# A causal mask by VectorE inside its row maximum, and a head's score tail beside the next head's masks

## The reference

```python
scores = jnp.einsum('bhqd,bhkd->bhqk', q, k) / np.sqrt(hd)
scores = scores + _alibi_causal_mask(S, scores.dtype)   # k <= q: -(q - k), else -1e30
probs = jax.nn.softmax(scores, axis=-1)
out = jnp.einsum('bhqk,bhkd->bhqd', probs, v)
```

## Time and profile before

| | |
|---|---|
| Median of 3 runs | 1567.94 us (1562.91 to 1567.96) |
| Span of the profiled execution, first to last instruction | 1560.2 us |
| Between the median and the span | 7.7 us |
| TensorE busy | 1472.0 us, 94% |
| TensorE weight loads | 946.3 us, 61% |
| VectorE busy | 1277.9 us, 82% |
| ScalarE busy | 1147.2 us, 74% |
| GpSimd busy | 858.0 us, 55% |

### The profile page before, as it was taken

The page is one execution under the profiler, slowest core; times in us unless marked ns, Lnnn a source line. Parts: engine busy times, 40 slices in busy tenths (PEclk is TensorE's granted clock), DMA queues, the critical chain, the costliest instruction groups (busy, mean ns, idle before and its releaser), DMA issues.

```text
span 1560.2 us, 56229 instructions
## 1 busy us (share of the span) xinstructions
PE 1472.0 (94%) x21476; PEld 946.3 (61%) x21476; DVE 1277.9 (82%) x3030; ACT 1147.2 (74%) x2464; POOL 858.0 (55%) x924
## 2 busy tenths in 40 slices
PE   6888999999999999999999999999999999999996
PEld 5555656666666666666666666656666656666653
DVE  6777888888888888888888888888888888888836
ACT  2477777778777777777877877777777777777762
POOL 2124556556556556655655665565665565566454
PEclk9799999999999999999999999999999999999988
DMA  5344555555455555455555545555545555554521
GB/s 170 99 150 127 171 156 173 152 170 157 149 178 155 175 153 166 143 168 167 157 180 152 160 146 170 166 160 157 165 142 167 175 150 178 154 169 139 157 73 50
DMA packets 197298, 239.73 MB, mean 154 GB/s; under 512 B 22462, under 2 KB 147782, under 8 KB 197030
## 3 DMA queue, kind: packets, MB, share of 16 engines
q1 hardware_dynamic: 196972, 236.07, 49.4%
q10 hardware_dynamic: 64, 0.07, 0.0%
HBM read 134.25 MB, written 100.73 MB: 151 GB/s over the span
## 4 chain that ended last, share of the span: by engine, by line
PE 62%; DVE 10%; DMA 9%; issue 6%; SPq 6%; ACT 3%; POOL 2%; POOLq 0%; DVEq 0%; ACTq 0%
PE ps L599 26%; PE ps L753 11%; PE ps L748 8%; PE ps L807 6%; DMA qk_d<-qk_st 5%; PE ps L802 5%; DVE mxp L1089 3%; DMA kz<-qk_d 2%; PE ps L768 2%; PE ps L662 2%; SPq L412 2%; DVE ve_c L1014 1%; DVE zr L1101 1%; DVE st_c L1000 1%; SPq L429 1%
## 5 line engine op out<-in xcount | busy, mean ns | idle before, releaser
L1089 DVE TENSOR_REDUCE mxp<-ps 128x4 f32<-128x512 f32 (+1 forms) x1536 | 842.8, 592 | 160.5 <-PE ps L768 155.6
L863 ACT ACTIVATE prob<-ps 128x512 f32<-128x512 f32 (+1 forms) x1536 | 732.6, 525 | 121.8 <-PE ps L753 116.4
L753 PE MATMUL ps<-qs,kz 50*128 50x128 f16 (+2 forms) x3584 | 405.9, 240 | 12.9 <-DVE mxp L1089 10.5
L768 PE MATMUL ps<-kz,qs 49*128 49x128 f16 (+1 forms) x4096 | 410.5, 231 | 0.1
L753 PEld LDWEIGHTS ps<-qs,kz 50*128 50x128 f16 x3584 | 261.4, 94 | 88.7 <-ACT prob L863 31.1
L768 PEld LDWEIGHTS ps<-kz,qs 49*128 49x128 f16 x4096 | 286.3, 95 | 3.8 <-DVE mxp L1089 1.8
L1347 POOL TENSOR_TENSOR om<-oc,rz 128x512 f32<-128x512 f32 x62 | 77.4, 1270 | 329.9 <-DMA rz<-rz_d 329.9
L807 PE MATMUL ps<-prob,va 128*32 128x384 f32 (+2 forms) x3072 | 237.6, 381 | 0.0
L748 PE MATMUL ps<-mk 64*128 64x256 bf16 x1024 | 198.6, 274 | 36.0 <-DMA kz<-qk_d 11.3
L802 PE MATMUL ps<-prob,va 128*32 128x128 f32 x4096 | 209.6, 277 | 0.6 <-DVE qk_st L1021 0.6
L764 PE MATMUL ps<-mk 64*128 64x256 bf16 x1024 | 201.0, 276 | 5.4 <-DVE mxp L1089 3.4
(11 more groups left out here) (157 smaller groups left out, 2870.6 us busy)
## 6 DMA issues: line engine op xcount, KB each, us to landing
qk_d<-qk_st SPq DMA_DIRECT2D x128, 256.0 KB, 2.8
ou_d<-ou SPq DMA_DIRECT2D x124, 256.0 KB, 2.3
qs<-qk_d SPq DMA_DIRECT2D x256, 96.0 KB, 2.4
kz<-qk_d SPq DMA_DIRECT2D x256, 96.0 KB, 2.5
xa<-in_L_attn_x SPq DMA_DIRECT2D x32, 512.0 KB, 5.2
qk_d<-qk_st SPq DMA_DIRECT2D x128, 128.0 KB, 3.4
xc<-in_L_attn_x SPq DMA_DIRECT2D x32, 512.0 KB, 4.1
oc<-ou_d SPq DMA_DIRECT2D x31, 512.0 KB, 4.9
```

The source lines that it names most:

```text
L753: x_ = mm(bank[:, col:col + w * P], kz[rows, h // 2, kt * P:(kt + 1) * P], qs[rows, h // 2, qt * P:(qt + w) * P], start=(n > 0), stop=(n > ...
L768: x_ = mm(bank[:, col * P:(col + w) * P], qs[rows, h // 2, qt * P:(qt + 1) * P], kz[rows, h // 2, kt * P:(kt + w) * P], start=(n > 0), sto ...
L863: nc.scalar.activation(prob[:, h % 8, at:at + w], ps[:, ST + n, 0:w], ACT.Exp, scale=1.0 / FS).then_inc(s["exp_done"], 1)
L1089: v.tensor_reduce(mxp[:, g % 2, at, first:first + apart * (BLOCKS[n] - 1) + 1:apart], bank.rearrange("p (m k) -> p m k", k=P), AX.X, ALU.m ...
```

## The change

- TensorE no longer adds a mask to the row scores. Row scores come in four whole tiles, one for each block of 128 queries, each with all its keys: 256 columns (bank 0), 512 (bank 1), 384 and 128 (bank 2). They take 4 matmuls instead of 10.
- VectorE adds the mask and takes the maximum of a tile in one instruction, `tensor_tensor_reduce` with add and max, four for each head. It reads the scores from PSUM and the mask from SBUF, writes the masked scores to a new tile `masked` (bf16), which nothing reads, and the maximum of each row straight into `mxt`. `mxp` and the four `rmax` steps of a batch are gone. `mt` waits for the last maximum of its group by `mx_read`.
- The tail of a head's transposed scores (256 columns, chunk 2) moves from part 2 of its own slot to part 0 of the next, between the two masks of the next head. ScalarE's exp of it comes first in the next slot.
- The constant mask has 1024 columns instead of 768.

```diff
-        MOVES = [6, 2, 2]
-        ROWS_AT = [[(0, 0, 1, 0), (1, 1, 1, 1), (2, 2, 1, 2), (3, 3, 1, 3)], [(3, 0, 3, 1), (2, 1, 1, 0)],
-                   [(1, 0, 1, 0), (2, 0, 1, 1)]]
+        ROW_TILES = [[(1, 0)], [(3, 0)], [(2, 0), (0, 3 * P)]]
+        MASKED = {3: 0, 2: 4 * P, 0: 7 * P, 1: 8 * P}
...
             def mt(b, n):
                 dst = to("mt", n, b)
-                wait(pe, "mxt_ready", b * 4 + n + 1)
+                wait(pe, "mx_read", b * 48 + 12 * (n + 1))
...
+            def row_score(b, pos, n, m):
+
+                h = pos ^ 1
                 rows = slice(HALF * (h % 2), HALF * (h % 2) + MX_ROWS)
...
+                qt, col = ROW_TILES[n][m]
+                w = (qt + 1) * P
+                x_ = mm(ps[:, MX + n, col:col + w], qs[rows, h // 2, qt * P:(qt + 1) * P],
+                        kz[rows, h // 2, 0:w], start=True, stop=True)
+                if m == len(ROW_TILES[n]) - 1:
                     x_.then_inc(s["mx_ready"], 1)
...
+            def masks_part(i, t):
+
+                bm, pos = max_at(i, t)
+                bp, hp = head_before(i, t)
+                if live(i):
...
+                    wait(pe, "exp_done", i * 48 + 3 * t - 2)
+                    mask(t, 0)
+                if live(bp):
+                    score(bp, hp, 2, 0)
+                if live(i):
+                    mask(t, 1)
+                if live(bm):
...
+                    wait(pe, "mx_read", bm * 48 + 3 * pos - 2)
+                    row_score(bm, pos, 0, 0)
+
+            def diagonal_part(i, t):
+
+                bm, pos = max_at(i, t)
+                if live(i):
+                    score(i, t, 0, 0)
+                if live(bm):
+                    wait(pe, "mx_read", bm * 48 + 3 * pos - 1)
+                    row_score(bm, pos, 1, 0)
+                if live(i):
+                    for m in range(1, 4):
+                        score(i, t, 0, m)
+
+            def past_part(i, t):
+
+                bm, pos = max_at(i, t)
+                if live(i):
+                    wait(pe, "exp_done", i * 48 + 3 * t - 1)
+                if live(bm):
+                    wait(pe, "mx_read", bm * 48 + 3 * pos)
+                for m in range(2):
+                    if live(i):
+                        score(i, t, 1, m)
+                    if live(bm):
+                        row_score(bm, pos, 2, m)
...
+            def exp_part(i, t, n):
+
+                b, h = (i, t) if n else head_before(i, t)
+                if live(b):
+                    exp(b, h, (n + 2) % 3)
...
-                bank = ps[:, MX + n, 0:BLOCKS[n] * P]
-                first, apart = MX_AT[n]
-                v.tensor_reduce(mxp[:, g % 2, at, first:first + apart * (BLOCKS[n] - 1) + 1:apart],
-                                bank.rearrange("p (m k) -> p m k", k=P), AX.X, ALU.max).then_inc(s["mx_read"], 1)
-
-            def rows_max(b, g):
-                wait(dve, "mx_read", b * 48 + 12 * (g + 1))
-                wait(dve, "mt_ready", b * 4 + g - 3)
-                v.tensor_reduce(mxt[:, g, :], mxp[:, g % 2].rearrange("p h (m k) -> p (h m) k", k=4), AX.X,
-                                ALU.max).then_inc(s["mxt_ready"], 1)
+                wait(dve, "mx_read", b * 48 + 3 * pos + n - 2)
+                if pos % 4 == 0 and n == 0:
+                    wait(dve, "mt_ready", b * 4 + g - 3)
+                for qt, col in ROW_TILES[n]:
+                    w = (qt + 1) * P
+                    x_ = v.tensor_tensor_reduce(masked[:, MASKED[qt]:MASKED[qt] + w], ps[:, MX + n, col:col + w],
+                                                mk[:, S - w:S], 1.0, -3e38, ALU.add, ALU.max,
+                                                mxt[:, g, 4 * at + qt:4 * at + qt + 1])
+                x_.then_inc(s["mx_read"], 1)
```

More of the change, by code:

```diff
@@ L66 @@
 DVE_AT = {
-    0: [(0, "rmax", 1, 0), (0, "ot", 0, -2), (3, "bn_c", 0, -2), (3, "ot", 1, -2)],
+    0: [(0, "ot", 0, -2), (3, "bn_c", 0, -2), (3, "ot", 1, -2)],
     1: [(3, "bn_c", 1, -2)],
@@ L77 @@
     12: [(3, "zs", 2, -2)],
-    13: [(1, "zs", 3, -2), (1, "rmax", 0, 1)],
+    13: [(1, "zs", 3, -2)],
 }
@@ L165, in build @@
         vst = sb("vst", [P, QT, D], F32)
-        mxp = sb("mxp", [P, 2, 4, 16], F32)
+        masked = sb("masked", [P, 10 * P], BF16)
         mxt = sb("mxt", [P, 4, 16], F32)
@@ L740, in moe, with mask @@
                 products(dst, pairs).then_inc(s["moe_ready"], 1)
+            def mask(h, u):
+                half = slice(HALF * (h % 2), HALF * (h % 2) + HALF)
+                mm(ps[:, ST, :].rearrange("p (t k) -> p t k", t=QT)[:, :, HALF * u:HALF * u + HALF], mask_key(u)[half],
+                   EYE[half].rearrange("p (t k) -> p t k", t=QT), start=(u == 0), stop=False)
             def score(b, h, n, m):
                 rows = slice(HALF * (h % 2), HALF * (h % 2) + ST_ROWS)
-                half = slice(HALF * (h % 2), HALF * (h % 2) + HALF)
@@ L746, in score @@
[L746 to L753, removed]
-                            qs[rows, h // 2, qt * P:(qt + w) * P], start=(n > 0), stop=(n > 0 or m == 5))
@@ L755, in score @@
-                if m == (MOVES[n] if n < 2 else 1) - 1:
+                kt, qt, w = CHUNK[n][m]
+                col = sum(c[2] for c in CHUNK[n][:m]) * P
+                last = m == len(CHUNK[n]) - 1
+                x_ = mm(ps[:, ST + n, col:col + w * P], kz[rows, h // 2, kt * P:(kt + 1) * P],
+                        qs[rows, h // 2, qt * P:(qt + w) * P], start=(n > 0), stop=(n > 0 or last))
+                if last:
                     x_.then_inc(s["st_ready"], 1)
-            def row_score(b, pos, h, n, m):
+            def row_score(b, pos, n, m):
+                h = pos ^ 1
@@ L793, in weigh @@
+            def both(i, t, n):
+                (masks_part, diagonal_part, past_part)[n](i, t)
             def weigh(b, g):
@@ L821, in drain @@
             def drain():
+                wait(pe, "exp_done", NB * 48 - 3)
+                score(LAST, H - 1, 2, 0)
                 weigh(LAST, 3)
@@ L938, in one @@
                 for t in range(SLOTS):
-                    play(i, t, ACT_END if i == LAST else ACT_AT, steps, lambda i, t, n: live(i) and exp(i, t, n))
+                    play(i, t, ACT_END if i == LAST else ACT_AT, steps, exp_part)
             hf_a_, hh_a_ = turned("ta", "ta_ready", 0, hf_a, hh_a, "hfa_ready", "hha_ready", "hla_ready",
@@ L954, in drain @@
             def drain():
+                exp(LAST, H - 1, 2)
                 sums_out(LAST, 3)
@@ L1449, in constants @@
     row = at % HALF
-    keys = [np.where(at[None, :] < row[:, None] + HALF * u, NEG, 0.0) for u in range(2)]
     queries = [np.where(at[None, :] > row[:, None] + HALF * u, NEG, 0.0) for u in range(2)]
     eye = np.tile(np.where(row[:, None] == np.arange(HALF)[None, :], 1.0, 0.0), (1, 4))
-    mask = np.concatenate([*keys, *queries, eye], axis=1).astype(np.float32)
+    future = np.where(np.arange(-3 * P, P)[None, :] > at[:, None], NEG, 0.0)
+    mask = np.concatenate([future, *queries, eye], axis=1).astype(np.float32)
     kaug = np.full((2, 8, 512), FS, np.float16)
```

55 lines of the change are left out of this document (16 added, 39 removed).

## The result

The kernel after takes 1604.42 us (median of 4 runs, 1602.89 to 1605.07) against 1566.55 us for the one before: ratio 1.0249, 95% interval 1.0224 to 1.0275. The forecast was 1606 us. The number is right by luck, and most of the reasons behind it are wrong: the price per head that the forecast gave VectorE isn't there, and a cost that it took as nothing is.

A forecast was written before the change was run, and what follows sets the result against it. TensorE paced the longest stretch, and VectorE would become the longer there. +1.1 us a batch x 31 = +34, plus 3 and 1.5 once, made +38 us and 1606 us; likeliest case 1580 to 1650, 8-in-10 range 1515 to 1700.

The forecast's parts named there:

- What leaves TensorE: Score matmuls: the old third part of a head goes, saving TensorE 0.11 to 0.17 us a head.
- What VectorE gets: Row maxima: a head costs VectorE 1.90 us instead of 1.54 (bounds 1.61 and 2.54), by a separate short instruction per tile.
- Stretch A: Batch part from 718.24 to 743.94, paced by TensorE: VectorE becomes the longer, 26.4 us, +0.7 a batch.
- first rival: Whole kernel: the maximum costs VectorE nothing extra, 1.61 us a head, TensorE stays the bound; 1505 to 1530 us, chance 0.28.
- Stretch B: Batch part from 743.94 to 753.21, TensorE and VectorE alternating: dearer maxima before the q and k products, +0.4 us.
- Stretch C: Batch part from 753.21 to 763.89, waiting on stores and loads: VectorE's extra work is covered by DMAs, no change.
- What is moved: Tail's exp first in ScalarE's next slot: ScalarE, busy 35.56 of 45.65 us, takes it; 0 us taken.
- VectorE busy over 93%: Sign for the forecast in the profile after: VectorE's busy share, 82% before, rises over 93%.
- its wait under 50 us: Sign for the forecast in the profile after: VectorE's wait for row scores falls from 155.6 us to under 50.
- slots that were 2.28 us apart: Sign for the forecast: these slot starts move further apart, since VectorE needs 1.90 us and its side work in each.
- no short instruction in the trace: Sign for the first rival, together with TensorE without waits in stretch A.
- dear rival: VectorE's second output is dear: 2.15 us a head gives 1689 us, the bound of 2.54 gives 1850; chance 0.12.

The follow-up runs named there:

- e4: Changed kernel with only the fused maxima in four tiles, the tail kept in its own slot and ScalarE's order as before; 1577.02 us, ratio 1.0091.
- e5: On e2, VectorE's layer-norm step ag_c of slot 2 moved from place 2 to place 3, behind the slot's last maxima; 1575.54 us, ratio 1.0050.
- e11: On e7, both layer-norm-statistics tensor_scalar instructions of VectorE replaced by tensor_reduce, GpSimd's add kept; 1525.36 us, ratio 0.9729.
- e12: The kernel before with only the edit of e11; 1558.81 us, ratio 0.9942.
- e2: Changed kernel with ScalarE's evictions hf_c and hh_c of slot 4 moved from place 1 to place 2, behind the diagonals' exp; 1564.67 us, ratio 1.0009.
- e10: The kernel before with only the tail moved between the next head's masks, its exp first in ScalarE's next slot; 1715.77 us, ratio 1.0939.
- e7: On e2, TensorE's first transposes (t2) of slot 4 moved from place 1 to place 2, behind the diagonals; 1556.72 us, ratio 0.9919.
- e3: Changed kernel with a short extra VectorE reduction of two values ahead of each of the 2048 fused tiles; 1670.25 us, ratio 1.0681.
- e8: On e7, layer-norm tensor_scalar instructions of VectorE replaced by a tensor_reduce and a subtract on GpSimd; 1622.81 us, ratio 1.0341.

## Why the prediction was right in its number and wrong in its reasons

- **What leaves TensorE: right, at its lower end.** The forecast had 0.11 to 0.17 us a head. The slots that TensorE bounds are 0.10 to 0.13 shorter.
- **What VectorE gets: wrong.** The step that failed is "I take the stream with the short instruction, 1.90 us a head". The short instruction exists, 82 ns long, but it starts together with the next tile and takes no turn of its own: 1.64 us a head, 0.26 us a head less than forecast, 4.2 us a batch. The stream's price was right: 0.61, 0.48, 0.34 and 0.21 us for the four tiles, forecast 0.603, 0.469, 0.335 and 0.201. The rule of the Trainium skill that an operation with accumulator is two instructions is borne out; that each takes its turn was the forecast's addition.
- **Stretch A: wrong in sign.** +0.7 us was forecast. Cut at masks, A is slots 8 to 15, 0 and 1 (up to 1.07 us), B the rest up to a little behind slot 5's masks, C what is left. Windows of after, cut at the masks of slots 8, 2, 5 and 8 (columns as in the earlier trace rows):

```profile
738.51:762.88 24.37, 23.92 (x313) 14.89 (x313) 21.47 (x92) 19.90 (x45) 14.93 (x15) 1.00 0.44 142
762.88:773.81 10.93, 8.28 (x111) 4.61 (x112) 9.69 (x39) 8.69 (x17) 9.94 (x13) 1.00 0.37 104
773.81:786.73 12.92, 12.20 (x149) 7.49 (x150) 8.76 (x41) 7.30 (x17) 2.22 (x3) 0.87 0.74 216
```

  By the table, these ten slots take 24.38 us instead of 24.73 (-0.35), slots 2 to 4 take 10.93 instead of 8.99 (+1.94), slots 5 to 7 take 11.90 instead of 12.22 (-0.32). In the first stretch TensorE is still busy for all but 0.45 us. The gain that the first rival had there, 1.1 to 1.8, isn't whole either: TensorE saves some 0.11 a slot, but slot 8 gives 0.53 of it back. There TensorE waits 0.38 us for an exp that now stands behind `z0`, the slot 4 mechanism in small.
- **Stretch B: right in place, wrong in size and cause.** +0.4 was forecast, for dearer maxima in front of the q and k products; +1.9 came. Slot 3's 0.69 is in the place that the forecast named, as e4 and e5 show, though not by the cost per head: VectorE's part 2 has 512 columns instead of 256 and stands behind a step that GpSimd holds. Without the hold slot 3 is 4.18 in the fused kernel (e11) and 3.85 in the one before (e12). So 0.33 of the 0.69 is the wider part 2, and 0.36 is that the same hold costs 0.61 there and 0.25 before. Slot 4's 1.49 isn't VectorE's at all.
- **Stretch C: nothing was forecast.** Two things that the forecast didn't have work against each other: 0.77 less in front of slot 8, 0.45 more in slots 5 and 6. In the batches at full clock these two slots take 7.64 us, 0.22 less than before; the half clock adds 0.66 on average.
- **What is moved: wrong, and the main miss.** The step is "ScalarE has 35.56 of 45.65 us busy and takes it". The busy share isn't the question for an engine that works in order. Moving the tail's exp to the front moved every other exp one part back, behind whatever stood at the place between. The forecast looked at slot 7 for such a meeting and not at slot 4, where the table has two long steps at place 1. e2 shows that this one meeting is worth as much as the whole +39 us, and e10 that it doesn't need the fused maxima. TensorE's place in slot 4 was missed too: 0.52 us of it, by e7.
- **The total** agreed by luck. The forecast's +1.1 us a batch was VectorE's. The measured +1.27 is slot 4's 1.49 (ScalarE and TensorE), 0.69 in slot 3 (VectorE), 0.45 and 0.42 in slots 5, 6 and 8, less 0.77 in slot 7 and 1.01 in the other slots together. Had the forecast's price per head been right as well, the two costs would have stood together: that is e3, 1670 us. The first rival, "TensorE stays the bound", had VectorE's price right (1.61, and it named 1.83 as the point that decides) and failed in its time by the same miss on ScalarE. With the meeting removed (e2) the kernel ties the one before, still short of that rival's 1505 to 1530; e11 reaches it with two more edits, of which the one in the layer norms is no part of the change.
- **The tests** that the forecast named did their work. "VectorE busy over 93%" and "its wait under 50 us" both failed in the first rows read, and so gave the coincidence away; slots that were 2.28 us apart are 2.17 apart and not further. The sign for the first rival, "no short instruction in the trace", was badly chosen: the short instruction is there, and the tiles still have that rival's price.
- **One sum isn't uniform.** The forecast leaves VectorE 1.7 us idle in stretch A. The dear rival's 28.2 leaves 1.0 (5.03 + 10.33 x 2.15 is 27.2) and its bound of 2.54 leaves none, without a row for either. The rival didn't come, so nothing here rests on it.

## What to carry to other kernels

When a step moves in the order of an engine, list what each later step now stands behind, slot by slot, and who waits for it; the busy share of that engine says nothing of it. Price a second instruction by the distance between starts in a trace that has it; if there is none, work the sum out for both cases. When a small instruction has a long or wandering duration, compare its end with the ends of the other engines' instructions: here that was worth 31 us, more than the change with its order mended (e7, 12 us).

## What the runs showed of the hardware

- The accumulator's read (`DVE_READ_ACCUMULATOR2_ANT`, 82 ns, 2048 times) starts at the same time as the next fused tile. Four tiles of 256, 512, 384 and 128 columns take 1.64 us start to start, 0.01 us a tile more than the price worked out from the plain reductions of before (1.61).
- A float32 `tensor_scalar` of four values per partition on VectorE that started while a GpSimd instruction ran took up to 1.29 us (e4; means by kernel and step from 349 to 1129 ns), and ended with that instruction within 0.03 us wherever it is told above; with GpSimd idle it took 0.17, and a `tensor_reduce` in its place takes 0.16 beside a running GpSimd instruction. The rule of the Trainium skill cited at e8 agrees with each of these.
- GpSimd's `tensor_scalar` on 128x256 float32 takes 554 ns with (add, mult) and 1221 ns with (subtract, mult).
- The granted clock fell from 1.00 to 0.50 in 13 of 27 batches of after, behind slot 4's wait (TensorE busy for 0.76 of 2 us at 206 to 208), and stayed there for about 3.4 us at 212 to 216. The same wait of 1.48 us is in every batch, the low clock only in some; why stays open. e2, where slot 4 is 0.89 us shorter, has 19 steps of 1 us at 0.50 instead of 43, which points at the wait but isn't a test of it alone.
